# Output banks swapped, two sums moved behind W's low parts, y of tile 0 moved ahead of W's scale

## The reference, cut to what matters

```python
q1 = fake_quant(layernorm(x), x1_scale, x1_zp)      # x: 2 x 512 x 1024
q2 = fake_quant(ctx_4096, x2_scale, x2_zp)          # 2 x 1024 x 1024
x = x + matmul(q1, q2)
y = layernorm(x)
logits = y @ W_router.T                             # 8 experts
topk_p, topk_i = top_k(softmax(logits), 2); topk_p = topk_p / sum(topk_p)
combine = sum(one_hot(topk_i, 8) * topk_p[..., None], axis=1)
h = einsum('nd,erd->ner', y, A_stack) * combine[..., None]
lora_out = einsum('ner,eor->no', h, B_stack) * 2.0
x = x + y @ W_base.T + b_base + lora_out
```

## Time and profile before

| | |
|---|---|
| time, median of 3 runs | 172.09 us (172.09 to 172.15) |
| the profiled execution | 172.12 us, span 170.3 us |
| granted TensorE clock | 1.00 of full speed |
| busy share of the span | TensorE 93%, VectorE 71%, ScalarE 44%, POOL 36% |

### The profile page before, as it was taken

The page is one execution under the profiler, slowest core; times in us unless marked ns, Lnnn a source line. Parts: engine busy times, 40 slices in busy tenths (PEclk is TensorE's granted clock), DMA queues, the critical chain, the costliest instruction groups (busy, mean ns, idle before and its releaser), DMA issues.

```text
span 170.3 us, 2631 instructions
## 1 busy us (share of the span) xinstructions
PE 158.8 (93%) x945; PEld 86.0 (51%) x945; DVE 121.3 (71%) x275; ACT 74.1 (44%) x100; POOL 61.2 (36%) x141
## 2 busy tenths in 40 slices
PE   6997898899999987999797999999999999999993
PEld 3553344345545345465363564555555456456582
DVE  7993939999989899949989908907816835814821
ACT  3196509799998991065306105205305304400000
POOL 8905476887943000054066072073064040000000
PEclk9999999999999999999999999999999999999999
DMA  4999999999930000001430360360360360360311
GB/s 115 391 417 414 408 406 411 409 411 408 408 134 2 0 0 4 0 0 31 92 127 2 62 184 0 65 185 0 62 185 4 62 185 0 62 185 4 125 73 50
DMA packets 19452, 25.89 MB, mean 152 GB/s; under 512 B 13552, under 2 KB 13808, under 8 KB 19440
## 3 DMA queue, kind: packets, MB, share of 16 engines
q1 hardware_dynamic: 19296, 25.73, 43.2%
q10 hardware_dynamic: 144, 0.00, 0.0%
HBM read 18.38 MB, written 4.19 MB: 133 GB/s over the span
## 4 chain that ended last, share of the span: by engine, by line
PE 67%; DVE 22%; POOL 4%; issue 3%; ACT 3%; DVEq 0%; ACTq 0%; POOLq 0%
PE ps L839 33%; PE ps L799 10%; PE ps L953 6%; PE ps L829 5%; PE ps L790 2%; PE ps L822 2%; PE ps L820 2%; PE ps L821 2%; DVE xs L541 2%; DVE w_lo L606 2%; ACT w_hi L370 2%; DVE cw L654 2%; DVE top_f L646 1%; PE ps L784 1%; DVE bnx L472 1%
## 5 line engine op out<-in xcount | busy, mean ns | idle before, releaser
L839 PE MATMUL ps<-w_hi,yt_hi 128*128 128x512 f16 x112 | 33.4, 380 | 1.8 <-DVE w_lo L606 1.8
L839 PE MATMUL ps<-w_hi,yt_lo 128*128 128x512 f16 x112 | 33.3, 379 | 0.0
L839 PE MATMUL ps<-w_lo,yt_hi 128*128 128x512 f16 x112 | 33.3, 379 | 0.0
L799 PE MATMUL ps<-a,a_t 128*128 128x512 f16 x128 | 31.2, 379 | 2.3 <-DVE a_t L534 1.5
L406 ACT ACTIVATE gate<-gate,ar_undo 128x1 f32<-128x1 f32 x8 | 2.4, 295 | 51.7 <-DVE gate L643 51.7
L331 ACT ACTIVATE a<-stage,prm,inv_s 128x1024 uint8<-128x1024 f32 x16 | 19.4, 1241 | 9.2 <-DMA stage<-in_ctx_kv 9.0
L263 POOL TENSOR_SCALAR root<-mvy 128x1 f32<-128x1 f32 (+1 forms) x7 | 1.5, 218 | 58.4 <-DVE mvy L466 37.5
L642 DVE MAX8 top<-ps 128x8 f32<-128x8 f32 x8 | 1.4, 173 | 26.6 <-PE ps L822 26.6
L799 PEld LDWEIGHTS ps<-a,a_t 128*128 128x128 f16 x128 | 11.9, 97 | 16.2 <-DVE a_t L534 3.0
L839 PEld LDWEIGHTS ps<-w_hi,yt_lo 128*128 128x128 f16 x112 | 11.0, 98 | 13.2
L839 PEld LDWEIGHTS ps<-w_lo,yt_hi 128*128 128x128 f16 x112 | 10.9, 98 | 13.2
(11 more groups left out here) (147 smaller groups left out, 293.9 us busy)
## 6 DMA issues: line engine op xcount, KB each, us to landing
stage<-in_ctx_kv SPq DMA_DIRECT2D x16, 512.0 KB, 13.2
stage<-in_w_t SPq DMA_DIRECT2D x8, 512.0 KB, 10.5
xs<-in_x SPq DMA_DIRECT2D x7, 512.0 KB, 13.1
out_dram<-xs SPq DMA_DIRECT2D x7, 512.0 KB, 3.0
ar_raw<-in_ar_t SPq DMA_DIRECT2D x1, 544.0 KB, 16.3
xs<-in_x SPq DMA_DIRECT2D x2, 256.0 KB, 3.7
b_raw<-in_b_t SPq DMA_DIRECT2D x1, 512.0 KB, 11.3
bias_sb<-in_bias SPq DMA_DIRECT2D x1, 512.0 KB, 12.0
```

The lines of the kernel that those rows point to most:

```text
L799: last = nc.tensor.matmul(ps[:, s1_bank(t) + h, :], a1_t[:, t % 4, k, :], a2[:, n, h * H:(h + 1) * H], start=k == 0, stop=k == K - 1)
L839: ins = nc.tensor.matmul(ps[:, OUT_BANK[p] + h, :], part, rhs[:, k, h * H:(h + 1) * H], start=k == 0 and part is hi and rhs is w_hi, stop= ...
```

## The change

- OUT_BANK becomes [4, 0] and LAST_BANKS (0, 1, 2): even tiles now write banks 4 and 5, odd ones 0 and 1.
- TensorE: the transposes of y(0) stand behind the peak of W, ahead of tile 7's products. Tile 0's wide steps no longer wait for sum 6; narrow(0) moves behind tile 1's step 0, with the waits for sums 6 and 7; the transpose of hc(0), narrow(1) and lora(0) each stand one step k later.
- ScalarE: y(0) and its split come ahead of W's high parts, split_ar between the fourth and the fifth of them, y(1) behind it. y(2) and its rounding stand ahead of gate_weight(1).
- VectorE: the split of y(0) ahead of W's low parts, split_ar between the fourth and fifth, sums 6 and 7 behind split_yt(1), the statistics of y(2) ahead of gate 0.
- POOL: scale_y of tile 2 ahead of the wait for b_lo.
- SP: the transposes of y(2) wait for narrow(0) and no longer for lora(0).

```diff
--- before.py
+++ after.py
@@ -133,12 +133,12 @@
         PEAK_BANK = 6
         PEAK_W_BANK = 4
         YT_BANKS = slice(6, 8)
-        OUT_BANK = [0, 4]
+        OUT_BANK = [4, 0]
         AR_BANK = 2
         HCT_BANK = 3
         HCT = slice(0, P)
         LAST_PIECES = ((0, H), (H, H + H // 2), (H + H // 2, D))
-        LAST_BANKS = (4, 5, 2)
+        LAST_BANKS = (0, 1, 2)
         PEAKS = 2 + K
         FIRST = 2
         FIRST_ADDS = 2
@@ -202,7 +202,10 @@
                 sp.dma_start(stage[:, n % RING, :], src).then_inc(stage_in[n % RING], 16)
 
             def transpose_y(t):
-                sp.wait_ge(out_done, t - 1)
+                if t == 2:
+                    sp.wait_ge(ar_done, 1)
+                else:
+                    sp.wait_ge(out_done, t - 1)
                 sp.wait_ge(y_hi_ready, t - 1)
                 sp.dma_start_transpose(out=yt_hi[:, t % 2, :, :], in_=y_hi).then_inc(y_hi_turned, 16)
                 sp.wait_ge(y_lo_ready, t - 1)
@@ -314,9 +317,9 @@
             scale_y(0, 2)
             pool.wait_ge(w_diag_ready, 1)
             add_corr(2)
-            pool.wait_ge(b_lo_ready, 1)
             for t in range(3, T):
                 scale_y(t - 1, t)
+                pool.wait_ge(b_lo_ready, 1)
                 add_corr(t)
             scale_y(T - 1, T)
 
@@ -426,22 +429,26 @@
             make_corr(1)
             for k in range(4, K):
                 peak_w(k)
+            make_y(0)
+            split_first_yt()
+            for k in range(4):
+                split_w(k)
             split_ar()
-            make_y(0)
-            split_w(0)
-            split_first_yt()
-            split_w(1)
-            split_w(2)
             make_y(1)
-            for k in range(3, K):
+            for k in range(4, K):
                 split_w(k)
             split_yt(1)
             split_b()
             gate_weight(0)
             split_hct(0)
+            make_y(2)
+            round_y(2)
+            gate_weight(1)
             sum_row(0)
             sum_row(1)
-            for t in range(1, T):
+            split_hct(1)
+            sum_row(2)
+            for t in range(2, T):
                 gate_weight(t)
                 if t + 1 < T:
                     make_y(t + 1)
@@ -728,23 +735,20 @@
             take_a1t(7)
             peaks_w()
             scale_w()
+            split_first_yt()
+            for k in range(4):
+                split_w(k)
+            split_ar()
+            for k in range(4, K):
+                split_w(k)
+            split_yt(1)
             sum_x1(6)
-            split_w(0)
-            split_first_yt()
-            split_w(1)
-            split_w(2)
-            split_w(3)
-            split_ar()
-            split_w(4)
             sum_x1(7)
             dve.wait_ge(iota_ready, 1)
             nc.vector.tensor_copy(expert[:, :], expert_i[:, :]).then_inc(expert_ready, 1)
-            for k in range(5, K):
-                split_w(k)
-            split_yt(1)
+            statistics_y(2)
             dve.wait_ge(expert_ready, 1)
             gate_tile(0)
-            statistics_y(2)
             split_b()
             split_hct(0)
             gate_tile(1)
@@ -881,6 +885,8 @@
                         pe.wait_ge(w_diag_ready, 1)
                         nc.tensor.matmul(ps[:, PEAK_W_BANK, 0:P], ones_b[:, :], diag[:, 2, :],
                                          start=True, stop=True).then_inc(w_peaks_done, 1)
+                        pe.wait_ge(ar_scale_ready, 1)
+                        transpose_y(0)
                     product(t, k)
                     if t == TB:
                         if k == 0:
@@ -892,14 +898,10 @@
                         nc.tensor.matmul(ps[:, PEAK_BANK, 0:2 * P], ones_b[:, :],
                                          diag[:, 0:2, :].rearrange("p g n -> p (g n)"),
                                          start=True, stop=True).then_inc(ar_peaks_done, 1)
-                    if t == T - 1 and k == 3:
-                        pe.wait_ge(ar_scale_ready, 1)
-                        transpose_y(0)
                     if t + 1 < T and k == 4:
                         transpose_a1(t + 1)
 
             keep_busy(2, 5)
-            pe.wait_ge(x1_summed, T - 1)
             pe.wait_ge(first_half_lo, 1)
             for k in range(K):
                 if k == K // 2:
@@ -908,19 +910,20 @@
                 wide(0, k, False)
                 if k == 3:
                     transpose_y(1)
-                if k == 5:
+
+            pe.wait_ge(yt_lo_ready, 2)
+            pe.wait_ge(x1_summed, T - 1)
+            for k in range(K):
+                wide(1, k, False)
+                if k == 0:
                     pe.wait_ge(x1_summed, T)
                     pe.wait_ge(ar_lo_ready, 2)
                     narrow(0)
-
-            pe.wait_ge(yt_lo_ready, 2)
-            for k in range(K):
-                wide(1, k, False)
-                if k == 1:
+                if k == 2:
                     transpose_hc(0)
-                if k == 2:
+                if k == 3:
                     narrow(1)
-                if k == 3:
+                if k == 4:
                     pe.wait_ge(b_lo_ready, 1)
                     lora(0, stop=True)
                 if k == 6:
```

## The result

The changed kernel takes 170.51 us (median of four, 170.49 to 170.85), the kernel before 172.09; the ratio is 0.9912 with an interval of 0.9895 to 0.9929. The profiled execution took 170.51 with a span of 168.7, against 172.12 and 170.3: 1.6 us less.

The account below looks back on a forecast made before the run. TensorE was taken to bound the kernel, with only its idle time before tile 3 to win. Losing 0.48 us up to narrow(1) but shortening gate 1's cast by 2.05 puts hct_lo(1) 1.57 earlier: 172.1 - 1.57 = 170.5, range 168.9 to 171.3.

Parts of the forecast that it names:

- Parts 1 and 2: Up to narrow(1): y of tile 0 ahead of W's scale, banks swapped, sums later; together 0.48 us lost.
- the loss of 0.48: TensorE up to narrow(1): its end moves from 75.66 to 76.14, despite 1.8 us of old holes removed.
- the holes of 0.45 and 0.77: New TensorE waits: 0.45 us before tile 0's step 4, 0.77 before tile 1's first step, for sum_x1(6).
- Part 3: Gate 1: POOL's add ends 0.36 us before VectorE's cast, which gets 2.05 shorter; SP's changed waits cost 0.
- rival D: ScalarE's queue: gate_weight(1) behind make_y(2) waits for a late scale_y(2); slower than before, 172.8 us; chance 0.05.
- The sum: From gate 1 on: hct_lo(1) at 82.83 instead of 84.40, everything behind 1.57 us earlier, total 170.5.
- The whole later pattern hangs on hct_lo(1): Behind gate 1: TensorE's tile 2 and POOL's later adds keep their distance from hct_lo(1), so all moves by 1.57 us.
- My sentence in case of a late TensorE: Tile 2's gate: if TensorE arrives later than hct_lo(1), the gate is later and POOL's add surely starts first; no size given.
- Rival B: Tile 2's gate: VectorE's eight-column add starts before POOL's add, hc isn't late, 1.37 us less; 169.2 us; chance 0.32.
- Rivals C and E: POOL's add ends after gate 1's cast starts, 171.3 us, chance 0.07; or another wait replaces hct_lo(1), 172.1, chance 0.04.

Follow-up runs that it names:

- the run without the hold: Changed kernel with one more wait on POOL: add_corr(4) waits for tile 2's hc; 169.35 us, ratio 0.9847.
- POOL's wait put back: Changed kernel with one edit undone: POOL waits for b_lo before scale_y(2) again; 174.37 us, ratio 1.0123.
- the gate part alone: Kernel before with only the gate orders changed on POOL, VectorE and ScalarE (scale_y(2), statistics_y(2), y(2) and its rounding earlier); 170.75 us, ratio 0.9922.
- the matmul part alone: Changed kernel with the gate orders on POOL, VectorE and ScalarE undone; banks, TensorE, W's order, sums and SP stay changed; 174.05 us, ratio 1.0164.
- The run with hc(1) transposed earlier: Kernel before with only the gate orders changed, plus transpose_hc(1) one step k earlier (behind k == 5 instead of 6); 170.71 us.

## Why the prediction was right, point by point

The forecast was 170.5, measured are 170.51. The steps, as predicted and as found in the rows above:

| step | predicted | after |
|---|---|---|
| transposes of y(0) start | 50.45 | 50.46 |
| first low part of W | 53.66 | 53.72 |
| tile 0's step 4 on TensorE | 61.60 | 61.71 |
| tile 1's step 0, behind sum 6 | 67.55 | 67.62 |
| maximum of gate 0 | 70.48 | 70.60 |
| transpose of hc(0) | 73.09 | 73.24 |
| add of tile 3 on POOL | 74.20 to 76.59 | 74.40 to 76.76 |
| maximum and cast of gate 1 | 76.34, 76.95 | 76.32, 76.93 |
| hct_lo(1) | 82.83 | 82.83 |
| lora(1) | 83.17 | 83.17 |

**Parts 1 and 2** hold to 0.15, each handover a little longer than taken. But the agreement to 0.02 at gate 1, and with it that of the time to 0.01, is luck: two errors cancel. The transpose behind a hole was taken to cost 0.33, its duration; the step to the next matmul is what counts, and that is 0.16 after 91.13 in the changed kernel (the run without the hold: 0.11, 90.00 to 90.11). The 93.04 of the earlier trace rows is where the record of the transpose at 92.71 ends; in the timeline of the kernel before the next matmul starts at 92.87:

```profile
92.87 0.59 PE L839 MATMUL ps<-w_hi,yt_hi 128*128 128x512 f16 x2
```

The 0.17 too much made up for 0.15 of handovers. The items given for the loss of 0.48 don't add up to it (1.29 and the new holes less 1.8 is 1.15): the 1.8 of the earlier trace rows counts from the end of a record, the new holes from step to step. By steps the four old holes are 1.8 and four times 0.16 (0.59 less 0.43), 2.5, and then the 0.48 comes out; found is 0.46 (narrow(1) ends at 76.12). In the same way the holes of 0.45 and 0.77 show in the rows as 0.34 and 0.57.

**Part 3** was right in its mechanism and too generous in its slack: b_lo took 1.22 and not 1.17, POOL woke up at 74.40, and the add cleared the cast by 0.17, not 0.36. That the coupling over ScalarE's queue (rival D's place) is real, and what it costs, is shown by POOL's wait put back: 2.9 us of waiting in gate 1.

**The sum.** That the change's value is in the gates and not in the four waits of the earlier trace rows is shown by the two halves: the gate part alone 1.35 faster, the matmul part alone 2.0 slower, both 1.58 faster. The matmul part brings 0.24 once the gate part is there.

**"The whole later pattern hangs on hct_lo(1)"** is too strong. It is so as long as gate 2 keeps its distance too, which it did here because TensorE stood waiting for hct_lo(1) before and after. The run with hc(1) transposed earlier separates the two, and the end did not follow hct_lo(1). My sentence in case of a late TensorE (POOL is surely first) was right in these two, though with no more than 0.01 and 0.07 to spare (88.46 against 88.47 with the gate part alone, 87.93 against 88.00 with hc(1) earlier).

**Rival B** had the right mechanism, the price of 1.37 was 0.2 too high (0.33 for the transpose again; 1.16 found), and none of the four runs shows it. The pattern did not keep its distance to the hundredth: the reciprocal at 87.57 waited 0.18 and came 0.40 behind the instruction before it, where in the kernel before it came 0.25 behind (88.74 to 88.99), so POOL was 0.16 ahead of the eight-column add and not on a par. I don't know why it waited; a POOL instruction ran beside it in both. In the kernel before, where both stand at 89.95, the race does go either way, as its run with a profile at 170.93 shows. Against those faster runs of the kernel before the change is worth 0.4 us, not 1.58, because they lack the hold at tile 2 and the changed kernel has it: the gate part alone and the kernel before then differ by 0.2. The prediction took the upper outcome for the only one, since the three times shown were all of it; it should have named the second time of the kernel before as part of rival B.

**Rivals C and E** did not come: nothing took the place of hct_lo(1), and no wait for y(2)'s transposes shows at 84.68. But C's mechanism is real, and the changed kernel missed it by 0.17: the last small instruction of scale_y(2) started at 72.93 and b_lo at 73.10. With the gate part alone b_lo started at 72.23 and took 1.22, and the small instruction that started behind it took 1.13, where in the changed kernel it took 0.19 (72.65):

```profile
72.36 1.13 POOL L290 TENSOR_TENSOR root<-mvy,y_scale 128x1 f32<-128x1 f32 x1
```

It cost nothing there, since POOL's add still ended 0.39 ahead of the cast.

## What to carry to other kernels

Two tiny instructions of 0.17 us were each worth more than 1 us because a long POOL add from SBUF had begun just ahead of them (at tile 2 shown by runs, at gate 1 read from the rows): look for short instructions with long durations, and for the POOL instruction with the same end. Here such a hold was taken away by a wait, by a delay of 0.3 us, and by an operand in PSUM. The kernel before, whose two starts lie on a par, had two times; compare a change with the outcome that has the same hold. Holes on the bounding engine ahead of the last wait brought nothing here until that last wait moved; moving work to fill them without moving it made this kernel slower.

## What the runs showed of the hardware that I had not expected

- A hole of TensorE of 2.60 us was followed by the lower clock: granted 0.52 from 87.0 to 90.5, then 1.00 again, in the profiled run with POOL's wait put back; in the matmul part alone (hole of 2.65) it was 0.62 from 87.0 to 90.5, then 1.00. It did not follow each time: one of the four runs with POOL's wait put back, of which there is no trace, had a mean of 1.00. Holes of up to 0.98 from 48 us on in the other kernels left it at 1.00.
- POOL's add holds an instruction with one SBUF tile of eight columns (2.25 for the cast, 2.38 and 2.32 for the two that make c2 and c1), but not a tensor_scalar or a reciprocal of a single column. Under POOL's add from 50.27 to 52.62 the changed kernel's VectorE ran five of the one and, at 51.29, one of the other (0.16), all at 0.14 to 0.20; the last of them:

```profile
51.68 0.14 DVE L608 TENSOR_SCALAR scale<-scale 128x1 f32<-128x1 f32 x1
```

  The Trainium skill, page "SBUF — State Buffer", section "Who interferes with whom", names copies, casts and tensor_scalar among those that can contend, if they run in a two-port mode. No row shows the mode; the cast and the tensor_scalar of eight columns were held, those of one column weren't.
- The other way round a single column is no protection: VectorE's b_lo (two SBUF tiles, 1.22) held a POOL instruction of one column for 1.13 with the gate part alone.
- Who starts first decided to a hundredth: VectorE was held when POOL's add stood 0.01 ahead (88.46 against 88.47, the gate part alone), and not when it stood 0.01 behind (90.02 against 90.01, the kernel before run again).
